# Waits between groups of four row scatters and gathers on GpSimd, in a kernel of two transformer layers with routed experts

## The chip, the cores and the metric

The kernel runs on one core of a Trainium2 chip. The metric is the device time of one execution in microseconds. A core has TensorE (PE in the profile), VectorE (DVE), ScalarE (ACT), GpSimd (POOL) and SyncE (SP), which run their own instruction queues in order and wait for each other on semaphores, and 16 DMA engines that all queues share.

## The reference

Input is x, 8 sequences of 512 tokens of 128 values. Two layers follow, each `x = x + ga * attention(h)` and then `x = x + gb * ffn(h)`, with `h = layernorm(x) * (1 + c) + s`, where shifts, scales and gains come from a small matrix product of a condition vector for each sequence.

- Layer 0: linear attention (16 heads of 8), then a mixture of 8 experts. For each token a softmax over 8 logits gives the two largest; each chosen expert computes `gelu(xn @ W1 + b1) @ W2 + b2` with 512 hidden values, and the two results are summed with normalised weights.
- Layer 1: softmax attention (8 heads of 16, each with values of 128 columns, the heads summed), then 8 experts of one 128x128 matrix, of which each token takes one.

The reference computes all experts for all tokens and masks. The kernel sorts the tokens by expert instead.

## The kernel before, in words

All work is in pairs: four pairs of two sequences, 1024 tokens, held as 8 row tiles of 128 tokens (NT = 8). Stages have names of kind.pair.part, and the order of the stages on every engine is written out by hand in the table ORDERS, one list for each engine (PE, ACT, DVE, POOL, and SP for the DMAs that SyncE issues). An engine takes its list in order; a stage that waits holds up all that stand behind it on this engine.

For the two-expert layer of pair i:

- VectorE computes, from TensorE's ranks (brk), the slot of each token and choice in a sorted buffer (posi, L1144). 23 tiles of 128 slots, each of one expert, hold the 2048 rows.
- bsc.i.0 to bsc.i.3 on GpSimd (L690): 16 indirect DMAs, four in each part, write the rows of z2 into xs (slots_in) in HBM, 128 rows of 512 bytes each. Each adds 16 to sc_out as it lands.
- bxl.i.j on SyncE (L530): waits until all 16 have landed (`sc_out >= 256 * (i + 1)`) and loads four tiles back. bw (L521) loads one expert's weights for each tile from the same in-order queue.
- bxt (transpose, L1496), bh (first product, L1503; gelu on ScalarE, L846), by (second product, L1511; copy on ScalarE, L854) on TensorE.
- byo (L540) stores the results to yd (slots_out) in HBM; bga.i.0 to bga.i.3 on GpSimd (L701): 16 indirect DMAs, four in each part, gather the rows back into yt, and count in ga_in[j], one semaphore for each part.
- bcm.i.j on VectorE (L1150, L1155) waits for ga_in[j] and combines; bcb (L1163, L1164) adds to x. Then come cn1 to cn4 (norms, partly on GpSimd: L658 to L665, L707, L708), and attention of layer 1: cpq (L1526), cpt on GpSimd (L736, L737), cto and cst (store and load of the split terms), s1 (L1538), mx on VectorE (L1198), s2 (L1554), exp on ScalarE (L887), pv (L1564).

For the one-expert layer, pairs 0 and 1 together go the same way: rsc.0.0 to rsc.0.3 (L722) scatter 16 blocks, rxl (L577) loads, rxt and rdx compute, rga.0.0 to rga.0.3 (L730) gather. Pairs 2 and 3 compute all experts (dx, L1607) and mask.

GpSimd's list has, around the parts: bsc.0.0 bn1.1.0 bsc.0.1 bsc.0.2 bsc.0.3; bsc.1.0 to bsc.1.3, then bga.0.0 to bga.0.3; bsc.2.0 bsc.2.1 bsc.2.2 bn1.3.0 bsc.2.3 cn1.0.0; bga.1.0 to bga.1.3, cpt.0.0; bsc.3.0 bsc.3.1 bsc.3.2 cpt.2.0 bsc.3.3, then bga.2.0 to bga.2.3, cpt.3.0; bga.3.0 to bga.3.3; rsc.0.0 to rsc.0.3, cpt.7.0; rga.0.0 rga.0.1 dx.2.0 rga.0.2 dx.2.2 rga.0.3. In the kernel before, only part 0 of a stream waits for anything; within a part and between the parts the DMAs are issued one behind the other.

Of the kernel before, what the change touches and what calls it, by code (L numbers as in the profile page):

```python
# [259 lines left out]
def build(nc, io, out):  # L260
    ctx = ExitStack()
    with ctx:
# [5 lines left out]
        def sem(name):  # L268
            return ctx.enter_context(nc.semaphore(name))
# [148 lines left out]
        def slot_rows(buf, g, n):  # L418
# [20 lines left out]
        ga_in = [sem(f"b_gathered{k}") for k in range(4)]  # L439
# [12 lines left out]
        r_row, r_mod, r_oh, r_rank, r_et, r_pos, r_sc, r_xt, r_mm, r_sum, r_wd = (  # L452
            sem("r_" + n) for n in ("rows_in_psum", "modulated", "one_hot", "ranks", "tile_experts", "slots", "scattered", "slots_turned",
                                    "expert", "x", "weights_stored"))
# [149 lines left out]
        def _(p):  # L604
# [41 lines left out]
            for kind, i, j in ORDER["POOL"]:  # L646
# [33 lines left out]
                if kind == "bsc":  # L680
                    if j == 0:
                        p.wait_ge(b_pos, i + 1)
                        p.wait_ge(b_z, i + 1)
                        if i == 0:
                            p.wait_ge(zx, 32)
                        if i >= 2:
                            p.wait_ge(b_xt, TG * (i - 1))
                    for x in range(4 * j, 4 * j + 4):
                        k, t = divmod(x, NT)
                        nc.gpsimd.indirect_dma_start(  # L690
                            xs[i % 2], bass.IndirectOffsetOnAxis(ap=posi[i][:, k, t:t + 1], axis=0),
                            z2[:, t, :], None).then_inc(sc_out, 16)
                if kind == "bga":
                    if j == 0:
                        for k in range(2):
                            p.wait_ge(ys_out[k], 16 * 3 * (i + 1))
                        if i:
                            p.wait_ge(b_cb, i)
                    for x in range(4 * j, 4 * j + 4):
                        t, k = divmod(x, 2)  # L700
                        nc.gpsimd.indirect_dma_start(  # L701
                            yt[:, k, t, :], None, yd[i % 2],
                            bass.IndirectOffsetOnAxis(ap=posi[i][:, k, t:t + 1], axis=0)).then_inc(ga_in[j], 16)
# [12 lines left out]
                if kind == "rsc":  # L716
                    if j == 0:
                        p.wait_ge(r_pos, 1)
                        p.wait_ge(r_mod, 2)
                    for x in range(4 * j, 4 * j + 4):  # L720
                        k, t = divmod(x, NT)
                        nc.gpsimd.indirect_dma_start(  # L722
                            xs[0], bass.IndirectOffsetOnAxis(ap=posi[0][:, k, t:t + 1], axis=0), zr[:, k, t, :], None).then_inc(r_sc, 16)
# [618 lines left out]
        def _(pe):  # L1342
# [10 lines left out]
            def keep_busy_aside(us, it):  # L1353

                _, gr, c = next((k for k in ORDER["PE"][ORDER["PE"].index(it):] if k[0] == "pv"), ("pv", len(values) // NC, 0))
                if c:
                    for _ in range(int(us / .23)):
                        nc.tensor.matmul(bank(7), nothing, rows, start=False, stop=False)
                else:
                    if gr:  # L1360
                        pe.wait_ge(c_ot, gr)
                    keep_busy(us, bank(7))
# [289 lines left out]
```

## Time and profile before

| | us |
|---|---|
| median of 3 runs | 782.74 |
| the runs | 777.67, 782.74, 787.64 |
| the profiled execution | 778.94 |
| its span, first to last instruction | 777.2 |
| busy: TensorE, VectorE, ScalarE, GpSimd | 632.0, 471.4, 392.1, 328.8 |
| mean granted TensorE clock | 0.905 |

The profiled execution is one of the program; what lies around its span is 1.7 us. Busy times are of instructions; waits, branches and DMA issues of SyncE do not count. "Releaser" is what ended a wait by the profile's semaphore events; "remote", and in the chain "another core or an unknown queue", stand where no instruction that fits was found. "Issue" is idle time for which no releaser is seen. Indirect DMAs stand as instructions of GpSimd, with the time in which it makes the descriptors, not that of the transfer. The matmuls of f32 operands stand as two instructions each. PEclk, the granted clock, is a share of 2.4 GHz; the other level, 1.2 GHz, is 0.50.

### The profile page before, as it was taken

To read this page: it belongs to the slowest core of one execution; us is meant where nothing else is said; L and a number is where in the kernel's file an instruction comes from. 1 tells how busy PE (TensorE), PEld (TensorE's weight loads), DVE (VectorE), ACT (ScalarE), POOL (GpSimd) and SP (SyncE) were. 2 spreads that over 40 slices of the span, in tenths; PEclk is the share of its full clock that TensorE was granted. 3 is DMA by queue.
4 is the path that set the end of the run, shared out by engine and by line. 5 is a ranking of instruction groups with operands and counts; after the bars stand their busy time and mean duration, and the time that the engine had idled before them with its cause. 6 is when DMAs were issued, how large, how long until landed. Compare 5 with 4: busy or idle time off the path is not lost.

```text
span 777.2 us, 12004 instructions
## 1 busy us (share of the span) xinstructions
PE 632.0 (81%) x3825; PEld 395.8 (51%) x3825; DVE 471.4 (61%) x1275; ACT 392.1 (50%) x866; POOL 328.8 (42%) x363
## 2 busy tenths in 40 slices
PE   8979889759496984988573999967899939988974
PEld 5646479658486984766120668812233312442332
DVE  3498847503365412778361685466899727588897
ACT  3451338637253653557342876644775417655430
POOL 5112880540608734351474131361646461406523
PEclk9999989959788895999795999986999679999998
DMA  8100337636457793596344358610420422532021
GB/s 342 50 1 29 125 93 241 213 121 199 136 170 243 243 322 94 198 297 184 129 143 114 90 189 269 224 41 14 150 82 2 132 87 78 171 99 65 14 54 27
DMA packets 47806, 106.41 MB, mean 137 GB/s; under 512 B 7825, under 2 KB 22993, under 8 KB 46209
## 3 DMA queue, kind: packets, MB, share of 16 engines
q1 hardware_dynamic: 42192, 94.82, 38.2%
q0 software_dynamic: 5120, 10.50, 4.3%
q8 instruction: 31, 0.51, 0.3%
q10 hardware_dynamic: 432, 0.34, 0.2%
q14 instruction: 31, 0.25, 0.1%
HBM read 80.26 MB, written 25.17 MB: 136 GB/s over the span
## 4 chain that ended last, share of the span: by engine, by line
PE 45%; DVE 18%; another core or an unknown queue 13%; ACT 9%; issue 7%; DMA 3%; POOL 2%; SPq 2%; DVEq 0%; ACTq 0%; POOLq 0%
PE PS L1503 8%; PE PS L1511 7%; DVE mxs L1198 6%; PE PS L1564 5%; PE PS L1554 4%; PE PS L1538 4%; ACT bufa L887 3%; ACT bufb L846 3%; DMA bufb<-in_experts_dram 3%; PE PS L1351 2%; PE PS L1607 2%; PE PS L1526 2%; PE PS L1427 1%; PE PS L1496 1%
## 5 line engine op out<-in xcount | busy, mean ns | idle before, releaser
L1198 DVE TENSOR_REDUCE mxs<-PS 128x2 f32<-128x1024 f32 x128 | 151.7, 1219 | 81.4 <-PE PS L1538 43.5
L887 ACT ACTIVATE bufa<-PS 128x512 f32<-128x512 f32 x256 | 140.8, 601 | 111.0 <-remote 49.5
L846 ACT ACTIVATE bufb<-PS,bufb 128x128 f32<-128x128 f32 x368 | 102.7, 378 | 99.5 <-PE PS L1503 50.2
L1503 PE MATMUL PS<-bufb 128*128 128x128 f32 x736 | 104.2, 292 | 22.8 <-issue 11.7
L1511 PE MATMUL PS<-bufb 128*128 128x128 f32 x736 | 102.5, 289 | 19.2 <-ACT bufb L846 10.1
L1554 PE MATMUL PS<-stk 108*128 108x512 bf16 x256 | 88.5, 404 | 35.1 <-ACT bufa L887 30.3
L1503 PEld LDWEIGHTS PS<-bufb 128*128 128x128 f32 x736 | 95.9, 204 | 33.6 <-issue 18.4
L1511 PEld LDWEIGHTS PS<-bufb 128*128 128x128 f32 x736 | 95.3, 203 | 24.0 <-ACT bufb L846 12.7
L1538 PE MATMUL PS<-stk 96*128 96x512 bf16 x256 | 81.2, 404 | 28.8 <-issue 10.2
L690 POOL DMA_INDIRECT slots_in<-bufb x64 | 66.3, 1037 | 70.6 <-DVE bufb L1144 52.7
L701 POOL DMA_INDIRECT bufb<-slots_out,bufb x64 | 61.0, 954 | 59.4 <-issue 33.8
L1554 PEld LDWEIGHTS PS<-stk 108*128 108x128 bf16 x256 | 23.3, 99 | 106.8 <-ACT bufa L887 63.4
L1564 PE MATMUL PS<-bufa,vv 128*32 128x512 f32 x512 | 74.2, 654 | 0.3 <-ACT bufa L894 0.2
L1538 PEld LDWEIGHTS PS<-stk 96*128 96x128 bf16 x256 | 20.6, 100 | 72.8 <-DVE mxs L1198 27.8
L1351 PE MATMUL PS<-identb 128*128 128x512 bf16 x187 | 46.2, 393 | 2.2 <-POOL dm L614 2.2
L656 POOL TENSOR_TENSOR rstd<-rstd,mhalf 128x8 f32<-128x8 f32 x12 | 20.7, 1725 | 62.4 <-DVE rstd L972 62.3
L736 POOL CAST terms<-rest 128x1024 bf16<-128x1024 f32 x8 | 8.3, 1043 | 72.7 <-DVE rest L1184 72.7
L1607 PE MATMUL PS<-bufb 128*128 128x512 f32 x64 | 30.6, 605 | 2.9 <-DVE bufb L1310 2.5
L838 ACT ACTIVATE bufb<-PS,cols 128x512 f32<-128x512 f32 (+1 forms) x24 | 18.5, 770 | 25.7 <-PE PS L1496 19.6
L1351 PEld LDWEIGHTS PS<-identb 128*128 128x128 bf16 x187 | 18.9, 102 | 22.0 <-issue 3.5
L658 POOL TENSOR_TENSOR mom<-st 128x16 f32<-128x16 f32 x11 | 2.4, 216 | 60.9 <-DVE st L956 60.9
L1035 DVE SCALAR_TENSOR_TENSOR bufa<-bufa 128x512 f32<-128x512 f32 x8 | 5.2, 686 | 35.4 <-ACT bufa L808 35.4
(292 smaller groups left out, 983.1 us busy)
## 6 DMA issues: line engine op xcount, KB each, us to landing
bufb<-in_experts_dram SPq DMA_DIRECT2D x92, 514.0 KB
stk<-split SPq DMA_DIRECT2D x96, 128.0 KB
slots_out<-bufb SPq DMA_DIRECT2D x30, 256.0 KB, 2.4
bufb<-slots_in SPq DMA_DIRECT2D x25, 256.0 KB, 4.1
split<-terms SPq DMA_DIRECT2D x8, 768.0 KB
slots_in<-hb SPq DMA_DIRECT2D x2, 1536.0 KB, 9.8
X<-in_x_dram SPq DMA_DIRECT2D x4, 512.0 KB, 6.5
out_dram<-X SPq DMA_DIRECT2D x6, 256.0 KB, 3.5
```

The costliest lines, as they stand in the source:

```text
L690: nc.gpsimd.indirect_dma_start(xs[i % 2], bass.IndirectOffsetOnAxis(ap=posi[i][:, k, t:t + 1], axis=0), z2[:, t, :], None).then_inc(sc_out ...
L701: nc.gpsimd.indirect_dma_start(yt[:, k, t, :], None, yd[i % 2], bass.IndirectOffsetOnAxis(ap=posi[i][:, k, t:t + 1], axis=0)).then_inc(ga_ ...
L846: last = nc.scalar.activation(hs[:, n % HR, fc, :], ps[:, P * fc:P * fc + P], ACT.Gelu_apprx_tanh, bias=ws[:, n % WR, F + fc:F + fc + 1])
L887: nc.scalar.activation(probs[:, i % PR, j, :], psum("s2", i, j), ACT.Exp, scale=DH1 ** -0.5)\
L1198: nc.vector.tensor_reduce(mxs[:, gr % 2, 2 * j:2 * j + 2, h], psum("s1", i, j).rearrange("p (c n) -> p c n", c=2), axis=AX.X, op=ALU.max)\
L1351: nc.tensor.matmul(place, identb[:, :], rows, start=True, stop=True)
L1503: last = nc.tensor.matmul(ps[:, P * fc:P * fc + P], ws[:, n % WR, P * fc:P * fc + P], xq[:, q % 2, P * x:P * x + P], start=True, stop=True)
L1511: last = nc.tensor.matmul(y, hs[:, n % HR, fc, :], ws[:, n % WR, W2AT + D * fc:W2AT + D * fc + D], start=(fc == 0), stop=(fc == FC - 1))
L1538: last = nc.tensor.matmul(ps[:, S * (c % 2):S * (c % 2) + S], qst[b % 2][0:KS, h, P * c:P * c + P], kst[b % 2][0:KS, h, :], start=True, st ...
L1554: nc.tensor.matmul(ps, kst[b % 2][0:KM, h, P * c:P * c + P], qst[b % 2][0:KM, h, :], start=True, stop=True).then_inc(c_s2x, 1)
L1564: last = nc.tensor.matmul(bank(7)[32 * hh:32 * hh + 32, :], vv[:, b % 3, j, 4 * k + hh, :], probs[:, n % PR, hh, :], start=(j == 0), stop= ...
L1607: last = nc.tensor.matmul(ps[:, 512 * e2:512 * e2 + 512], xTd[i % 2][:, P * j:P * j + P], expT[:, 4 * e2:4 * e2 + 4, :].rearrange("p e d - ...
```

## The change

Three waits are added on GpSimd. The second, third and fourth part of a scatter of pairs 1 to 3 (bsc) wait until all DMAs of the stream so far have landed; the second to fourth part of each gather (bga) until the part before has; the second to fourth part of the last scatter (rsc) likewise. The first pair's scatter and the last gather (rga) are as before. Nothing else is changed.

```diff
--- before.py
+++ after.py
@@ -685,6 +685,8 @@
                             p.wait_ge(zx, 32)
                         if i >= 2:
                             p.wait_ge(b_xt, TG * (i - 1))
+                    elif i:
+                        p.wait_ge(sc_out, 256 * i + 64 * j)
                     for x in range(4 * j, 4 * j + 4):
                         k, t = divmod(x, NT)
                         nc.gpsimd.indirect_dma_start(
@@ -696,6 +698,8 @@
                             p.wait_ge(ys_out[k], 16 * 3 * (i + 1))
                         if i:
                             p.wait_ge(b_cb, i)
+                    else:
+                        p.wait_ge(ga_in[j - 1], 64 * (i + 1))
                     for x in range(4 * j, 4 * j + 4):
                         t, k = divmod(x, 2)
                         nc.gpsimd.indirect_dma_start(
@@ -717,6 +721,8 @@
                     if j == 0:
                         p.wait_ge(r_pos, 1)
                         p.wait_ge(r_mod, 2)
+                    else:
+                        p.wait_ge(r_sc, 64 * j)
                     for x in range(4 * j, 4 * j + 4):
                         k, t = divmod(x, NT)
                         nc.gpsimd.indirect_dma_start(
```

## Rows read from the trace of the kernel before

**Rows 1.** The page: TensorE's busy time; the chain that ended last, by engine.
```profile
...
PE 632.0 (81%) x3825; PEld 395.8 (51%) x3825; DVE 471.4 (61%) x1275; ACT 392.1 (50%) x866; POOL 328.8 (42%) x363
...
PE 45%; DVE 18%; another core or an unknown queue 13%; ACT 9%; issue 7%; DMA 3%; POOL 2%; SPq 2%; DVEq 0%; ACTq 0%; POOLq 0%
...
```

**Rows 2.** View of waits: engine and line, releaser, us in total, times, longest.
```profile
...
ACT bufa L887 <- remote: 49.5, 10, 13.5
ACT bufb L846 <- remote: 45.7, 7, 11.9
...
```

**Rows 3.** Timeline, ScalarE and VectorE: start, us, what [idle before, releaser].
```profile
...
155.71 0.67 ACT L838 ACTIVATE bufb<-PS,cols 128x384 f32<-128x384 f32 x1 [5.36 <-remote]
...
169.29 1.14 ACT L846 ACTIVATE bufb<-PS,bufb 128x128 f32<-128x128 f32 x4 [11.88 <-remote]
...
215.03 1.23 DVE L1063 TENSOR_TENSOR bufa<-PS,modb 128x1024 f32<-128x1024 f32 x1 [11.42 <-remote]
...
707.45 1.23 DVE L1198 TENSOR_REDUCE mxs<-PS 128x2 f32<-128x1024 f32 x1 [2.22 <-remote]
...
```

**Rows 4.** Timeline of TensorE: what those at 169.29 and 215.03 need.
```profile
...
156.44 2.08 PE L1503 MATMUL PS<-bufb 128*128 128x128 f32 x8 [4.59 <-ACT bufb L838]
...
201.74 3.75 PE L1454 MATMUL PS<-wa,xTa 128*128 128x128 f32 x16 [4.20 <-issue]
...
```

**Rows 5.** Timeline of GpSimd: single indirect DMAs.
```profile
...
99.31 0.96 POOL L690 DMA_INDIRECT slots_in<-bufb  x1 [0.30 <-issue]
...
147.70 0.96 POOL L690 DMA_INDIRECT slots_in<-bufb  x1 [0.30 <-issue]
...
165.37 0.95 POOL L690 DMA_INDIRECT slots_in<-bufb  x1 [0.30 <-issue]
...
235.09 2.06 POOL L690 DMA_INDIRECT slots_in<-bufb  x1 [0.30 <-issue]
...
286.87 0.94 POOL L701 DMA_INDIRECT bufb<-slots_out,bufb  x1 [0.30 <-issue]
...
710.08 0.96 POOL L730 DMA_INDIRECT bufb<-slots_out,bufb  x1
...
```

**Rows 6.** Timeline of SyncE's DMA queue and of VectorE: who waits for rows.
```profile
...
101.54 7.43 SPq L530 DMA_DIRECT2D bufb<-slots_in  x4
...
182.47 0.85 SPq L530 DMA_DIRECT2D bufb<-slots_in  x2
...
292.76 0.67 DVE L1150 SCALAR_TENSOR_TENSOR bufb<-bufb,hb 128x128 f32<-128x128 f32 x2 [17.80 <-DMA bufb<-slots_out,bufb]
...
318.00 2.02 DVE L1150 SCALAR_TENSOR_TENSOR bufb<-bufb,hb 128x128 f32<-128x128 f32 x2
...
```

**Rows 7.** Stretches: length, busy PE, PEld, DVE, ACT, POOL, granted clock, DMA share, GB/s.
```profile
...
422.00:506.00 84.00, 81.33 (x579) 58.02 (x579) 50.41 (x102) 62.84 (x154) 20.24 (x24) 0.96 0.57 179
...
146.00:171.00 25.00, 12.90 (x79) 11.80 (x78) 2.42 (x4) 5.92 (x20) 15.41 (x16) 0.75 0.48 163
192.00:215.00 23.00, 11.87 (x75) 11.01 (x74) 7.67 (x34) 6.67 (x12) 15.09 (x16) 0.74 0.43 140
231.00:256.00 25.00, 18.34 (x123) 17.28 (x123) 14.28 (x34) 10.33 (x32) 20.14 (x22) 0.83 0.76 242
283.00:307.00 24.00, 11.91 (x81) 11.35 (x79) 2.04 (x8) 6.89 (x19) 15.21 (x16) 0.76 0.45 154
365.00:383.00 18.00, 9.68 (x55) 2.89 (x53) 6.97 (x10) 7.15 (x13) 11.53 (x12) 0.84 0.57 190
394.00:422.00 28.00, 12.01 (x54) 3.15 (x53) 7.81 (x13) 6.12 (x11) 19.47 (x21) 0.69 0.60 178
506.00:532.00 26.00, 15.82 (x66) 3.53 (x67) 14.67 (x20) 9.34 (x18) 15.31 (x16) 0.78 0.15 41
618.00:641.00 23.00, 10.74 (x46) 3.12 (x50) 5.27 (x5) 4.50 (x9) 15.50 (x16) 0.72 0.35 108
697.00:717.00 20.00, 17.28 (x86) 5.01 (x86) 16.70 (x25) 11.02 (x21) 14.99 (x15) 1.00 0.17 44
...
```

## The prediction

> **What bounds the kernel now.** I read the page first: its busy shares, then its chain. TensorE is busy for 632.0 of 777.2 us, and no other engine is near that; the chain goes through TensorE for 45%, and for 13% through "another core or an unknown queue", though there is one core [rows 1]. 13.2% of 777.2 us is about 102 us, so that name has to be found. The view of waits gives it as "remote": ScalarE alone waited 49.5 us in 10 waits before its exp (L887) and 45.7 us in 7 waits before its gelu (L846) [rows 2]. The timeline tells when. I filtered it for "remote": 30-odd waits, and every one of them lies inside, or within 5 us behind, a run of indirect DMAs on GpSimd (the row scatters and gathers); none lies between 424 and 506, where GpSimd issues none. The reader is to see four of them [rows 3]: ScalarE's L838 at 155.71 after 5.36 us, a gelu at 169.29 after 11.88 us, VectorE's L1063 at 215.03 after 11.42 us, and a short one at 707.45.
>
> What they waited for had been computed. The gelu of 169.29 waits for eight matmuls of L1503 that began at 156.44 and took 2.08 us; L1063 of 215.03 waits for the projection of L1454, which began at 201.74 and took 3.75 us [rows 4]. So the matmuls were over at 158.5 and 205.5, and the news of it took 10.8 and 9.5 us. GpSimd's runs lie exactly there: 16 scatters from 146.34 (the second is at 147.70) to 165.37, which is one every 17.67 / 14 = 1.26 us [rows 5], and 16 gathers that end at 211.7. The waits end 1 to 4 us behind the last issue. My reading: while row moves follow each other without a pause, what TensorE signals to other engines comes late; I can't say through what.
>
> Two things show that a pause lets the signals through. The scatter of the first pair and that of the third are broken up: single issues last 1.8 to 2.06 us there (as at 235.09 [rows 5]) and GpSimd has other work in between; from 76 to 101 ScalarE has no remote wait, from 231 to 256 two short ones, 4.64 and 1.87 us. And the last gathers (L730) come as eight, then 2.8 us of sums, then four from 710.08 [rows 5]: during the eight there is a wait of 2.22 us [rows 3], during the four none. The lateness begins some 4 us into a run, at its fourth DMA: in the run of 146.34 the first remote wait is that which ends at 155.71, so it began at 150.35.
>
> The Trainium skill (SBUF — State Buffer, "SBUF: two separate sides") says that a DMA cannot be slowed by a compute op, and vice versa. By that rule the 102 us would have another cause and the change would give nothing: it is the second rival below. The trace does not follow it in this case, since the waits come and go with the runs.
>
> **What the change removes.** The windows price it [rows 7]. Eight runs, each with its tail (146:171, 192:215, 231:256, 283:307, 365:383, 394:422, 506:532, 618:641), last 192 us together, and TensorE is busy in them for 12.90 + 11.87 + 18.34 + 11.91 + 9.68 + 12.01 + 15.82 + 10.74 = 103.3 us: 88.7 us idle. Two rows say what would be left without the lateness. In the stretch 422:506 without row moves, TensorE is idle for 2.7 of 84 us, 3%: of 192 us that is 6 us, an upper end of 83 us gained. In 697:717, with the gathers in a group of eight and one of four, it is idle for 2.7 of 20 us, 13.6%: of 192 us 26 us, so 63 us gained. I take the second, since it is the row nearest to groups of four.
>
> The clock comes on top. The granted clock is 0.69 to 0.84 in the eight windows and 0.96 and 1.00 in the two others [rows 7]: TensorE falls from 2.4 to 1.2 GHz after it stood idle, and goes on at the lower level for some us. 103.3 us of busy time at a mean of 0.76 would be some 103.3 x (1 - 0.76 / 0.96) = 21 us shorter at most; half of it, 10 us, is my estimate, because part of the low clock falls on idle time and the exps and VectorE's maxima don't get faster. Bounds 0 and 21 us.
>
> **What it adds.** Waits in front of the second, third and fourth group: 3 for each scatter of pairs 1 to 3, 3 for each of the four gathers, 3 for the last scatter (L722): 24, of which the one before bsc.3.3 costs nothing, since 12 us of other work lie in front of it. Each puts a landing in the place of a pitch of 1.26 us. The lower end of a landing: the last scatter of the first pair starts at 99.31, and SyncE, which waits for all 256, issues its load at 101.54 [rows 5, 6]: 2.2 us, so 1.0 us more for each wait, 3 us for a run. The upper end: the fourth gather of pair 1 starts at 286.87 and VectorE, which waits for those four, starts at 292.76 [rows 5, 6]: 5.9 us, 4.6 us more a wait, 14 us a run. That one lies amid weight loads and amid the lateness itself, so I take 1.3 us: 23 x 1.3 = 30 us of waiting on GpSimd, 4 us a run. Those 30 us are not on the path by themselves. Behind a waiting bsc or bga on GpSimd's queue stand: the rest of that stream, bn1.3 and cn1.0 behind the third scatter (VectorE waits for their pow), cpt.0 behind the second gather, cpt.7 behind the last scatter. Who waits for the rows: SyncE's bxl, VectorE's bcm.
>
> Their slack: bxl.1.0 is issued at 182.47 [rows 6], 15 us after its last scatter landed (165.37 + 2.2); VectorE's bcm.1.1 begins at 318.00 [rows 6], 14 us after the last of its gathers landed (286.87 + 12 x 1.25 + 2.2 = 304). But this slack is in large part the stall: with TensorE 9 to 12 us further on, 2 to 5 us are left, and the run ends 4 us later, in bad cases 14. So I charge 0 to 2 us in each of the eight places and 15 us in all; bounds 0 and 40 us (five places at 8 us). The first pair's scatter is not touched, nor the last gathers. The gather of pair 2 (bga.2.0) still starts without a wait right behind bsc.3.3, a run of eight: about 4 us of lateness stays there, and is inside the 26 us.
>
> **The sum.** 63 + 10 - 15 = 58 us less. The profiled execution took 778.94 us with a span of 777.2, and would take 721; it lies 3.8 us under the median of the three runs shown, 782.74. On the median's level: 725 us. Its own range, from the bounds that go together: gain 83 + 21 - 5, 99 us, gives 684; gain 63 + 0 - 35 gives 755.
>
> **Rivals.** First: the pause is too short. What GpSimd pauses is one landing, about 1 us in which nothing is issued, where the gap before 710.08 was 2.8 us and the work between the parts of the scatter of 76 to 101 lasted 2 us. Then the groups run together for the signals, and only a third of the 63 us comes: 21 - 15, about 6 us, with the longer runs sharing the lateness: 777. For it: full recovery behind the long runs took up to 1.8 us after the landing. Against it: the single issue of 2.06 us at 235.09, only 1.1 us longer than usual, is enough for the gelus behind it. In between lies a half effect, 745 to 765.
>
> Second: the runs aren't the cause, the same minutes of the kernel would be slow for another reason (weights landing late), and the change does not do what it says. Then only the charge of the waits is left, 0 to 15 us: 790, no change within 2%. Against it: in 506:532 the DMA share is 0.15 and TensorE is idle for 10 us all the same [rows 7].
>
> Third, on the other side: the landings take the place of the stall. A landing under load is 5.9 us [rows 6], not 2.2; each run of 16 then lasts 20 + 3 x 4.6, 34 us, and SyncE's in-order queue, where all weight loads stand behind a bxl, waits for the scatters. It decides from the point where a run grows by more than its slack of some 15 us of now, or sooner if the lateness goes on beside the waits. Five of eight runs at 8 us and a fifth of the gain (14 us): 782.7 + 40 - 14, about 809.
>
> The Trainium skill (DMA: Bandwidth & Descriptors, "Rules for kernel authors") speaks against the change: issue the DMA early, wait on its semaphore late, the fixed cost overlaps; and it gives some 2.0 us of fixed cost for a DMA from GpSimd (section "Anatomy of one DMA"). The fixed cost agrees with the 2.2 us of [rows 5, 6]. By the rule alone the change would only add 23 waits, which is the third rival at its lower prices.
>
> **Chances.** My forecast 0.74 (684 to 755); half effect or too short a pause 0.14 (745 to 777); not the cause 0.06; landings instead of the stall 0.06. The range that should hold it 8 times in 10 reaches from 692 to 765. 2% of 782.74 is 15.7 us, about what a measurement of this kernel can tell from no change: faster below 767. Faster 0.86 (the forecast, and most of the half effect), same 0.08, slower 0.06.
>
> **What the profile after would show.** Remote waits in the view of waits fall from over 100 us to under 30, and "another core" in the chain from 13% to under 4%. GpSimd's timeline shows groups of four 1.26 us apart and a gap of 1.1 to 2 us (plus the 0.3) before the fifth, ninth and thirteenth. The PEclk line has no falls to 7 in those slices, and mean clock rises from 0.905 to about 0.95. TensorE's idle time in each former window is 2 to 4 us. I am wrong if these waits stay while the gaps are there (first rival), if they stay elsewhere (second), or if VectorE's L1150 and SyncE's L530 now wait for landings by 5 us or more each (third).

## The result and the profile after

The kernel with the waits takes 723.65 us (median of 4 runs, 718.42 to 729.92), that without them 782.62 us (4 runs, 777.67 to 787.64) on the same chip. The ratio is 0.9212 with a 95% interval of 0.9148 to 0.9275: faster by 8%. The profiled execution of after is the longest of its four, 729.92 us with a span of 728.2 us; that of before was 3.7 us under its median. So the two profiles stand 49.0 us apart in span and the medians 59.0 us, and everything read below accounts for the 49.

I read the page first: the span, TensorE's busy time, the granted clock in 40 slices and the chain.

```profile
span 728.2 us, 12004 instructions
...
PE 621.5 (85%) x3825; PEld 390.0 (54%) x3825; DVE 483.3 (66%) x1275; ACT 391.9 (54%) x866; POOL 328.6 (45%) x363
...
PEclk9999999999998899889998999999999699999998
...
PE 19%; DVE 11%; issue 5%; POOL 5%; DMA 4%; SPq 4%; ACT 1%; ACTq 0%; DVEq 0%; POOLq 0%
```

TensorE is busy for 10.5 us less than in [rows 1] (632.0) with the same 3825 matmuls, which I put down to the clock. It is idle for 106.7 us where it was 145.2: 38.5 us less. The two make the 49.0. "Another core or an unknown queue" is gone from the chain; but this chain reaches back only to 368.4 us, so it shows one half of the kernel, and the view of waits is the safer place. There the change shows from both sides (engine, line, tile, what it waited for: us in total, times, longest):

```profile
POOL bufb L705 <- DMA bufb<-slots_out,bufb: 36.5, 12, 4.5
...
POOL slots_in L692 <- DMA slots_in<-bufb: 28.0, 8, 5.3
...
DVE bufb L1156 <- DMA bufb<-slots_out,bufb: 25.5, 5, 9.5
...
PE PS L1509 <- DMA bufb<-in_experts_dram: 13.9, 6, 6.0
...
DVE mxs L1204 <- remote: 7.9, 4, 4.2
ACT bufb L844 <- remote: 7.8, 3, 2.8
...
ACT bufb L852 <- remote: 6.4, 4, 3.5
...
POOL slots_in L728 <- DMA slots_in<-bufb: 4.6, 3, 1.5
...
ACT bufb L860 <- remote: 3.8, 1, 3.8
...
ACT stk L886 <- remote: 3.2, 1, 3.2
...
ACT bufa L900 <- remote: 2.1, 1, 2.1
```

The lines marked "remote" sum to 31.2 us. In before the same lines sum to 165.9 us, 95.2 of them in the two of [rows 2] (the gelu is L852 now, the exp L893, which has none left). In exchange GpSimd stands at 23 of the 24 added waits for 36.5 + 28.0 + 4.6 = 69.1 us, 3.0 us each. Other landings are waited for longer. VectorE's first combine (now L1156) waited 17.8 us in one piece before [rows 6], and TensorE waited for expert weights 3.0 us, which are 13.9 now:

```profile
PE PS L1503 <- DMA bufb<-in_experts_dram: 3.0, 3, 1.7
```

(that is the same view of before; the matmul is L1509 after). One wait for a landing is new. VectorE's second norm (L986, called at L1091) writes the rows z2 of pair 2 over those that the scatters of pair 1 still read, so it waits until they have landed, and TensorE waits for it in turn:

```profile
177.72 2.14 DVE L986 TENSOR_SCALAR bufb<-hb,mom,rstd 128x128 f32<-128x128 f32 x8 [6.08 <-DMA slots_in<-bufb]
...
180.00 1.94 PE L1466 MATMUL PS<-identf,bufb 128*128 128x128 f32 x8 [5.82 <-DVE bufb L986]
```

The timeline shows the new rhythm of GpSimd, and where the last "remote" waits lie (start, duration, engine, line; in brackets the idle time before and its releaser):

```profile
150.42 0.96 POOL L692 DMA_INDIRECT slots_in<-bufb  x1 [0.30 <-issue]
...
155.09 0.96 POOL L692 DMA_INDIRECT slots_in<-bufb  x1 [3.71 <-DMA slots_in<-bufb]
...
163.72 0.96 POOL L692 DMA_INDIRECT slots_in<-bufb  x1 [3.89 <-DMA slots_in<-bufb]
...
212.26 0.94 POOL L705 DMA_INDIRECT bufb<-slots_out,bufb  x1 [0.30 <-issue]
213.51 1.31 POOL L692 DMA_INDIRECT slots_in<-bufb  x1 [0.30 <-issue]
...
215.68 0.58 ACT L860 COPY bufb<-PS 128x512 f32<-128x512 f32 x1 [3.85 <-remote]
```

ScalarE's operations of 155.71 (L838) and 169.29 (a gelu), which had waited 5 and 12 us [rows 3], have no such wait near them; the one "remote" wait of that stream is of 0.72 us, at 160.85. The one of 215.68 lies where the last four gathers of pair 0 (208.52 to 212.26) and the first four scatters of pair 2 (213.51 on) meet without a wait: a run of eight is left there. The windows follow, one for each of the eight streams with its tail and a quiet one (length, busy PE, PEld, DVE, ACT, POOL, granted clock, DMA share, GB/s), to be laid beside [rows 7]:

```profile
146.00:179.00 33.00, 25.12 (x198) 23.60 (x197) 6.17 (x16) 20.86 (x52) 15.41 (x16) 0.99 0.66 207
183.00:215.00 32.00, 27.60 (x218) 25.16 (x216) 21.59 (x80) 17.18 (x47) 17.32 (x17) 0.96 0.70 227
215.00:247.00 32.00, 25.55 (x183) 23.56 (x183) 9.82 (x24) 16.04 (x51) 17.83 (x24) 0.89 0.64 204
265.00:299.00 34.00, 31.51 (x230) 27.70 (x228) 11.51 (x42) 21.46 (x55) 17.70 (x18) 0.95 0.55 189
356.00:383.00 27.00, 21.71 (x104) 6.69 (x98) 18.96 (x23) 15.20 (x29) 18.66 (x18) 0.94 0.34 114
383.00:406.00 23.00, 18.46 (x111) 12.15 (x112) 13.41 (x24) 15.47 (x34) 13.10 (x14) 0.85 0.58 160
472.00:497.00 25.00, 21.05 (x114) 6.63 (x114) 22.06 (x40) 14.07 (x26) 14.09 (x15) 1.00 0.14 36
576.00:599.00 23.00, 19.52 (x93) 5.65 (x92) 13.85 (x20) 12.51 (x23) 14.36 (x15) 0.89 0.38 115
...
407.00:470.00 63.00, 61.17 (x455) 45.73 (x454) 38.03 (x75) 43.93 (x116) 17.61 (x23) 1.00 0.68 221
```

In the eight, TensorE is busy for 190.5 of 229 us, so idle for 38.5; before it was idle for 88.7 of 192. The windows are longer because the streams are. They gave 50.2 us; outside them idle time grew from 56.5 to 68.2 us, which is 11.7 us given back.

Late signals are not all that goes with the runs. TensorE itself is held up in them. Behind the projection of L1454 [rows 4] its next matmuls of before come singly, with idle time for which no releaser is seen, while the gathers are issued:

```profile
210.47 0.37 PE L1503 MATMUL PS<-bufb 128*128 128x128 f32 x1 [1.83 <-issue]
...
212.61 0.37 PE L1503 MATMUL PS<-bufb 128*128 128x128 f32 x1 [1.76 <-issue]
...
214.00 0.37 PE L1503 MATMUL PS<-bufb 128*128 128x128 f32 x1 [1.03 <-issue]
```

All lines of the view of waits that give TensorE's matmuls the releaser "issue" sum to 43.2 us in before and to 15.1 us in after.

### The profile page after: what moved, and what is told of

Its sections match the earlier page's. It is cut to its first block and busy times, and to the rows that moved or that the text cites. A ratio compares the mean times of both kernels' runs of the same rounds, so it can differ in the third digit from the quotient of the medians.

```text
span 728.2 us, 12004 instructions
## 1 busy us (share of the span) xinstructions
PE 621.5 (85%) x3825; PEld 390.0 (54%) x3825; DVE 483.3 (66%) x1275; ACT 391.9 (54%) x866; POOL 328.6 (45%) x363
## 5 line engine op out<-in xcount | busy, mean ns | idle before, releaser
L893 ACT ACTIVATE bufa<-PS 128x512 f32<-128x512 f32 x256 | 140.5, 601 | 70.5 <-PE PS L1560 46.0
L852 ACT ACTIVATE bufb<-PS,bufb 128x128 f32<-128x128 f32 x368 | 102.9, 379 | 74.7 <-PE PS L1509 62.0
L1509 PE MATMUL PS<-bufb 128*128 128x128 f32 x736 | 105.4, 295 | 26.3 <-DMA bufb<-in_experts_dram 13.9
L1509 PEld LDWEIGHTS PS<-bufb 128*128 128x128 f32 x736 | 96.6, 206 | 38.0 <-issue 24.4
L692 POOL DMA_INDIRECT slots_in<-bufb x64 | 64.7, 1011 | 81.3 <-DVE bufb L1150 37.3
L1560 PE MATMUL PS<-stk 108*128 108x512 bf16 x256 | 86.5, 396 | 17.3 <-ACT bufa L893 9.0
L1517 PE MATMUL PS<-bufb 128*128 128x128 f32 x736 | 98.1, 282 | 3.3 <-ACT bufb L852 2.5
L1517 PEld LDWEIGHTS PS<-bufb 128*128 128x128 f32 x736 | 91.5, 197 | 6.7 <-ACT bufb L852 4.3
L705 POOL DMA_INDIRECT bufb<-slots_out,bufb x64 | 62.1, 971 | 66.4 <-DMA bufb<-slots_out,bufb 36.5
L1570 PE MATMUL PS<-bufa,vv 128*32 128x512 f32 x512 | 71.8, 635 | 0.2 <-ACT bufa L900 0.2
L1357 PE MATMUL PS<-identb 128*128 128x512 bf16 x187 | 48.4, 408 | 2.2 <-POOL dm L614 2.2
L736 POOL DMA_INDIRECT bufb<-slots_out,bufb x16 | 15.4, 962 | 23.8 <-DMA slots_out<-bufb 19.5
L728 POOL DMA_INDIRECT slots_in<-bufb x16 | 15.5, 967 | 18.1 <-DVE bufb L1305 9.8
L1570 PEld LDWEIGHTS PS<-bufa,vv 128*32 128x32 f32 x512 | 10.5, 110 | 24.4 <-issue 21.8
```

The source lines that it names most:

```text
L692: nc.gpsimd.indirect_dma_start(xs[i % 2], bass.IndirectOffsetOnAxis(ap=posi[i][:, k, t:t + 1], axis=0), z2[:, t, :], None).then_inc(sc_out ...
L705: nc.gpsimd.indirect_dma_start(yt[:, k, t, :], None, yd[i % 2], bass.IndirectOffsetOnAxis(ap=posi[i][:, k, t:t + 1], axis=0)).then_inc(ga_ ...
L852: last = nc.scalar.activation(hs[:, n % HR, fc, :], ps[:, P * fc:P * fc + P], ACT.Gelu_apprx_tanh, bias=ws[:, n % WR, F + fc:F + fc + 1])
L893: nc.scalar.activation(probs[:, i % PR, j, :], psum("s2", i, j), ACT.Exp, scale=DH1 ** -0.5)\
L1357: nc.tensor.matmul(place, identb[:, :], rows, start=True, stop=True)
L1509: last = nc.tensor.matmul(ps[:, P * fc:P * fc + P], ws[:, n % WR, P * fc:P * fc + P], xq[:, q % 2, P * x:P * x + P], start=True, stop=True)
```

## Experiments

Each kernel is compared with the kernel before on the same chip. "Remote" is the sum of the lines with that name in the view of waits of its profiled execution; "landing waits" are GpSimd's own for its row moves. Times are medians, with the lowest and highest run in brackets. Unless a diff says otherwise, the edit is against the kernel after the change.

**Which streams carry the gain.** First the waits in the scatters of pairs 1 to 3 alone, the other two additions taken out.

```diff
                     elif i:
                         p.wait_ge(sc_out, 256 * i + 64 * j)     (kept)
-                    else:
-                        p.wait_ge(ga_in[j - 1], 64 * (i + 1))
-                    else:
-                        p.wait_ge(r_sc, 64 * j)
```

> Only the scatters of pairs 1 to 3 keep the waits; gathers and the last scatter run without. Lateness theory (an unbroken run of row moves on GpSimd holds up what TensorE signals): the stalls go in the three scatters alone, worth 12.1 + 6.7 + 8.3 of the 88.7 us of idle before, less what their waits cost: 760 to 770 us. If the gain came from one stream only (a rival), this one gives all of it (724) or nothing (783). Remote waits should be gone in the scatters and stand as before in the gathers.

764.13 us (762.65 to 768.3) against 776.28; ratio 0.9841 (0.9779 to 0.9903): 12 us. Remote 135.2 us, all of it but 0.15 us outside the three scatters. As expected.

Then the waits in the four gathers alone.

```diff
-                    elif i:
-                        p.wait_ge(sc_out, 256 * i + 64 * j)
                     else:
                         p.wait_ge(ga_in[j - 1], 64 * (i + 1))   (kept)
-                    else:
-                        p.wait_ge(r_sc, 64 * j)
```

> Only the four gathers keep the waits. Lateness theory: 11.1 + 12.1 + 16.0 + 10.2 us of idle time were theirs, 35 to 40 us come back: 743 to 750 us. Rival (the writes of the scatters into HBM are what holds up the signals): no gain, 780 us.

760.48 us (758.42 to 765.45), ratio 0.9807 (0.973 to 0.9885): 16 us, less than half of the 35 to 40 that I expected. Both ratios lie clear of 1, but neither interval lies wholly beyond 2%. Remote is down to 90.4 us, so the signals of the gathers come as foreseen; but VectorE's combine now waits for its rows:

```profile
DVE bufb L1152 <- DMA bufb<-slots_out,bufb: 45.2, 6, 28.6
```

17.8 us before [rows 6], 45.2 here. The lateness also moved on: the scatter of pair 2 follows the gather at once, still unbroken, and ScalarE's gelu at 240.25 waits 11.9 us there, where the longest such wait of this scatter was 4.6 us in before. Which of the two costs the gain was not run. The two parts give 28 us, the whole 59. The last scatter's waits alone were not run, so how much of the other 31 us is theirs and how much only comes when no stream is left unbroken stays open.

**Is it the number of row moves under way?** With groups of four that each wait for the last one, at most four are in flight. A gather may instead wait for the group before the last: up to eight in flight, and hardly a pause. Only the gathers have waits here.

```diff
-                    else:
-                        p.wait_ge(ga_in[j - 1], 64 * (i + 1))
+                    elif j > 1:
+                        p.wait_ge(ga_in[j - 2], 64 * (i + 1))
```

> Only the four gathers have waits, and each for the group before the last one (the third group waits for the first, the fourth for the second): no more than eight DMAs in flight, but hardly a pause. Compared with waits for the last group in the gathers alone (760, ratio 0.981). Pause theory: the first group has landed long before the third begins, GpSimd issues without a break, nothing is gained: 770 to 785 us. Rival (too many row moves in flight at once): as good as the waits in the gathers, 755 to 765 us.

778.21 us (771.67 to 784.03), ratio 0.9998 (0.9961 to 1.0035), remote 135.8 us. No landing wait of the gathers shows on GpSimd at all, the groups run together, and nothing is gained: where the waits hold nothing up, they are worth nothing. This remote sum is 30 us under that of before with the same span of 777.2 us, so differences of that size between two such sums mean little by themselves.

**How long may a group be?** A wait before every second row move, and one wait in the middle of the sixteen.

```diff
 groups of two (the same in the gather and in the last scatter)
                     for x in range(4 * j, 4 * j + 4):
+                        if i and x % 4 == 2:
+                            p.wait_ge(sc_out, 256 * i + 16 * x)
 groups of eight (the same in the gather and in the last scatter)
-                    elif i:
+                    elif i and j == 2:
                         p.wait_ge(sc_out, 256 * i + 64 * j)
```

> As the changed kernel, but a wait in front of every second DMA instead of every fourth. Lateness theory, with the lateness beginning some 4 us into a run: a run of 2 never gets there, so remote waits vanish, but GpSimd waits for 7 landings a stream instead of 3, some 2.7 us each, 11 us more a stream; I expect 720 to 735 us. If the lateness begins at once, groups of 2 gain further: under 715 us. If the longer streams are what ends last, over 740 us.

> As the changed kernel, but one wait only, in the middle of each stream. Lateness theory: each half of 10 us is stalled from its fourth us on, so about a third to a half of the gain stays: 745 to 760 us. If only the first pause mattered, or the number of landings per stream, it is 724 us; if a run of eight is as bad as one of sixteen, 775 us.

Groups of two: 777.13 us (773.85 to 781.11), ratio 1.0017 (0.9981 to 1.0052), no gain at all, where I had expected 720 to 735. Groups of eight: 739.82 us (737.13 to 741.03), ratio 0.9539 (0.9482 to 0.9597), a little better than expected. The first is the more telling. Its view of waits has not one "remote" line; what it has instead:

```profile
DVE bufb L1162 <- DMA bufb<-slots_out,bufb: 79.1, 13, 12.6
POOL bufb L709 <- DMA bufb<-slots_out,bufb: 74.5, 28, 6.5
...
POOL slots_in L694 <- DMA slots_in<-bufb: 49.4, 19, 5.1
...
PE PS L1515 <- DMA bufb<-in_experts_dram: 32.1, 7, 12.5
...
PE PS L1508 <- DMA bufb<-slots_in: 18.0, 3, 14.2
```

With another 11.9 us in the last scatter GpSimd is held up for 135.8 us in 54 waits. All 166 us of late signals are gone, and what the third rival foresaw stands in their place: rows land late for VectorE, and the queue behind SyncE's row loads lands late for TensorE. VectorE's second norm waits 16.4 us for the scatters, and the lines of TensorE with the releaser "issue" are down to 3.3 us. In groups of eight remote is 81.2 us and the landing waits are 20.6 us (7).

**Landing or pause?** In the next two nothing waits for a landing. GpSimd does one pow of 128x8 elements between the groups, into a tile that nobody reads, or two in a row.

```diff
+        idle = sb("idle", [P, NT])
...
                     elif i:
-                        p.wait_ge(sc_out, 256 * i + 64 * j)
+                        own.link(tt(idle[:, :], epst[:, :], mhalf[:, :], ALU.pow))
                     else:
-                        p.wait_ge(ga_in[j - 1], 64 * (i + 1))
+                        own.link(tt(idle[:, :], epst[:, :], mhalf[:, :], ALU.pow))
                     else:
-                        p.wait_ge(r_sc, 64 * j)
+                        own.link(tt(idle[:, :], epst[:, :], mhalf[:, :], ALU.pow))
```

> In the places of the added waits GpSimd does one power of a 128x8 tile, 1.65 us, and waits for its end; it waits for no landing. If a pause in the issuing is what lets TensorE's signals through, the remote waits fall nearly as far as in the changed kernel (31 us) and GpSimd is held up for 23 x 1.9 us instead of 69 us: 700 to 720 us. If it takes the landing (no row move in flight at some moment), which under load comes 3 to 5 us after the fourth, most of the gain in the weight-loading part is lost and the rest stays: 735 to 755 us.

> The same with two powers, 3.5 us. Pause theory: remote waits no higher than with one power, 23 x 1.8 us more on GpSimd, so equal to the changed kernel or slower: 710 to 725 us. Landing theory: now most landings fit into the pause and the time comes near to the changed kernel, 715 to 730 us, faster than with one power.

One pow: 701.91 us (698.56 to 704.12), ratio 0.9017 (0.8967 to 0.9068), below the interval of the change itself. Its page and GpSimd's timeline:

```profile
PE 613.3 (87%) x3825; PEld 384.4 (55%) x3825; DVE 476.7 (68%) x1275; ACT 391.8 (56%) x866; POOL 372.2 (53%) x387
...
PE 32%; POOL 19%; DVE 18%; issue 9%; DMA 7%; SPq 7%; ACT 6%; another core or an unknown queue 1%; DVEq 0%; POOLq 0%; ACTq 0%
```

```profile
148.14 0.96 POOL L694 DMA_INDIRECT slots_in<-bufb  x1 [0.30 <-issue]
149.13 1.68 POOL L691 TENSOR_TENSOR idle<-epst,mhalf 128x8 f32<-128x8 f32 x1
151.10 1.04 POOL L694 DMA_INDIRECT slots_in<-bufb  x1 [0.29 <-POOL idle L691]
```

From the end of the fourth issue to the start of the fifth it is 2.0 us (149.10 to 151.10) where the wait for the landing took 3.7 (151.38 to 155.09 in after). Remote is 17.1 us, not more than the 31.2 with the longer stop. So it is not the landing that helps; the landing is only a pause, and a dearer one than needed. The granted clock rises to 0.961.

Two pows: 742.69 us (741.8 to 743.68), ratio 0.9559 (0.9509 to 0.9608), where I had expected at most 730. Remote is 22.8 us, no better than with one. 24 pauses x 1.7 us are 41 us more on GpSimd, and the kernel is 40.8 us slower (TensorE is busy for 7 us of these, at a granted clock of 0.938): in this step a microsecond of stream cost about a microsecond. POOL is the largest share of its chain, 33%, and VectorE waits again:

```profile
DVE bufb L1160 <- DMA bufb<-slots_out,bufb: 38.8, 9, 9.7
```

**How short may the pause be, and how is it to be spread?** Three linked multiplications (0.78 us) in the place of the pow; the pow once in the middle of sixteen; and the short pause after every second row move, so that a stream has about as much pause as with the pow, in smaller pieces. The diffs are against the kernel with one pow.

```diff
 short pause
-                        own.link(tt(idle[:, :], epst[:, :], mhalf[:, :], ALU.pow))
+                        for _ in range(3):
+                            own.link(tt(idle[:, :], epst[:, :], mhalf[:, :], ALU.mult))
 pow in the middle alone
-                    elif i:
+                    elif i and j == 2:
 short pause every two: as the first, and
                     for x in range(4 * j, 4 * j + 4):
+                        if i and x % 4 == 2:
+                            for _ in range(3):
+                                own.link(tt(idle[:, :], epst[:, :], mhalf[:, :], ALU.mult))
```

> The pause of the kernel with one pow (1.68 us of work, 1.96 us from the end of the fourth issue to the start of the fifth, instead of 0.30) is cut to about half: three multiplications of 128x8 elements, 0.20 us each and linked, some 0.85 us, so 1.1 to 1.2 us between the groups. If any pause of about 1 us is enough for TensorE's signals, remote waits stay under 30 us and the shorter streams give another 0 to 10 us: 692 to 704. If the pause has to be near 2 us, remote waits come back to 50 to 120 us and the time is 715 to 750.

> One pow after the eighth row move of each stream instead of one after every fourth: the pause is the same, the runs between are 8 long. If lateness builds up from about the fourth DMA of a run, remote waits are near the 81 us of the kernel with one landing wait in the middle, GpSimd is held up for 10 us less than there, and the time is 725 to 740. If a pause as such is what counts, wherever it lies, remote waits are under 40 us and the time is 695 to 710.

> The short pause (three multiplications, 0.78 us of work) after every second row move instead of after every fourth. For 16 row moves this is 7 pauses of 0.78 us beside work, 0.76 us of extra gap each, 5.3 us, against 3 x 1.67 = 5.0 us in the kernel with one pow every four (701.9 us) and 2.3 us in that with the short pause every four (743.3 us, 92 us of remote waits). If lateness builds up with each row move and is paid back with the idle time of GpSimd's issue, whatever its form, remote waits are under 35 us and the time is 698 to 715. If a pause under 1 us gives nothing back and only long ones do, remote waits stay at 60 to 100 us and, with streams as long as with the pow, the time is 735 to 755.

Short pause every four: 743.34 us (740.42 to 747.02), ratio 0.9482 (0.9404 to 0.9559), remote 92.1 us; a gap of 1.08 us in place of 0.30 is too short for four row moves. Pow in the middle alone: 750.52 us (738.85 to 756.06), ratio 0.9605 (0.9524 to 0.9686), remote 81.7 us, as expected, but slower than my 725 to 740. One of its waits lies in the first eight gathers of pair 0 (182.02 to 191.8) and the pause behind them:

```profile
193.50 1.07 ACT L822 COPY xTa<-PS 128x512 f32<-128x512 f32 x2 [6.36 <-remote]
```

Short pause every two: 709.08 us (705.9 to 712.35), ratio 0.9094 (0.9019 to 0.9168). Its rhythm, and both of its "remote" lines:

```profile
147.76 0.96 POOL L697 DMA_INDIRECT slots_in<-bufb  x1 [0.30 <-issue]
148.73 0.79 POOL L695 TENSOR_TENSOR idle<-epst,mhalf 128x8 f32<-128x8 f32 x3
149.80 1.00 POOL L697 DMA_INDIRECT slots_in<-bufb  x1 [0.28 <-POOL idle L695]
```

```profile
ACT stk L899 <- remote: 3.1, 1, 3.1
...
DVE bufb L1329 <- remote: 0.7, 1, 0.7
```

The same short pause that left 92.1 us of late signals after every four leaves 3.8 us after every two. So it is not the length of the single pause that counts, but how much pause there is for how many row moves.

**The places that the change left out.** First the landing waits also in the scatter of pair 0, before the gather of pair 2, and in the last gather; then, against the kernel with one pow, a pow before the scatter and the gather of pair 2 and in the last gather.

```diff
 landing waits everywhere
-                    elif i:
+                    else:
                         p.wait_ge(sc_out, 256 * i + 64 * j)
 bga, j == 0
+                        if i == 2:
+                            p.wait_ge(sc_out, 1024)
 rga
+                    else:
+                        p.wait_ge(r_ga[(j - 1) // 2], 64 * ((j - 1) % 2 + 1))
 pow at the joins: in bsc and bga, j == 0
+                        if i == 2:
+                            own.link(tt(idle[:, :], epst[:, :], mhalf[:, :], ALU.pow))
 rga
+                    else:
+                        own.link(tt(idle[:, :], epst[:, :], mhalf[:, :], ALU.pow))
```

> The changed kernel with waits in the three places that it leaves out: the first pair's scatter, between the last part of the fourth scatter and the gather behind it, and the last gather. Theory: 4 to 8 of the 31 us of remote waits left lie behind the fourth scatter and go; the first pair's scatter has none to lose and starts everything behind it 6 to 9 us later, as no other expert work is there to hide it: 722 to 732 us against 717 to 724, slightly slower.

> Beside the pauses of the kernel with one pow every four, one at each place where two runs meet without one: before the scatter of pair 2 (behind the gather of pair 0), before the gather of pair 2 (behind the scatter of pair 3), and three in the last gather. If the remaining 17 us of remote waits come from those runs of eight, they fall under 10 us, and the time is 694 to 702; the last gather lies on the path, and its pauses (2 x 1.7 us) may take 3 us of it back: not over 706.

Landing waits everywhere: 724.43 us (723.52 to 725.25), ratio 0.9322 (0.9274 to 0.937); remote 10.8 us, landing waits 78.3 us (28). Pow at the joins: 705.73 us (700.62 to 708.28), ratio 0.902 (0.8956 to 0.9085); remote 10.7 us against 17.1. In both the late signals fall to some 11 us, and in neither does the time follow: the ratio of the second is that of one pow every four (0.9017), and its 706 us lie at my limit and not in the 694 to 702 that I had expected. The last places cost about what they give.

**The kernels that treat the eight streams alike, in one table.** "Added" is the time that a stream of sixteen grows by its pauses, each less the plain 0.30 us: for landing waits (69.1 - 23 x 0.30) / 23 = 2.7 us a wait in after, 2.6 in groups of eight, 2.2 in groups of two (135.8 us in 54 waits); for the others the gap in the timeline, 2.00 us with a pow, 1.08 with the short pause, 3.71 with two pows.

| kernel | added per stream, us | remote, us | ratio to before |
|---|---|---|---|
| before | 0 | 165.9 | 1 |
| pow in the middle | 1 x 1.7 = 1.7 | 81.7 | 0.9605 |
| short pause every 4 | 3 x 0.78 = 2.3 | 92.1 | 0.9482 |
| landing in the middle | 1 x 2.6 = 2.6 | 81.2 | 0.9539 |
| pow every 4 | 3 x 1.7 = 5.1 | 17.1 | 0.9017 |
| short pause every 2 | 7 x 0.78 = 5.5 | 3.8 | 0.9094 |
| landing every 4 (after) | 3 x 2.7 = 8.1 | 31.2 | 0.9212 |
| two pows every 4 | 3 x 3.4 = 10.2 | 22.8 | 0.9559 |
| landing every 2 | 7 x 2.2 = 15.5 | 0 | 1.0017 |

About 2 us added takes off half of the lateness, 5 us nearly all of it and a tenth of the time; within these two groups the ratios' intervals overlap, so no difference between the forms of the pause is shown. Beyond 5 us the time comes back with the stream's length. The change lies at 8 us, on the far side of the best.

## Why the prediction came right

**What bounds the kernel.** The reading was right. The "remote" waits belong to the unbroken runs of row moves: they went from 165.9 to 31.2 us with the runs cut, to 0 with runs of two, and stayed (135.8) when waits were there that held nothing up. I had said from over 100 to under 30. But "what TensorE signals comes late" was only part of it: TensorE's own idle time without a releaser goes the same way, 43.2 us before, 15.1 after, 7.6 with one pow every four, 3.3 in groups of two. By what path the row moves do this is still not shown, nor whether it is their issue on GpSimd or the transfers behind it; the runs show only that the delay comes and goes with unbroken issue. The Trainium skill (SBUF — State Buffer, "SBUF: two separate sides") holds that a DMA and a compute op can't slow each other; the costliest operations of ScalarE and VectorE did not get longer here (the exp 601 ns in both kernels, VectorE's maximum 1.22 us), but the news of one did come up to 12 us late [rows 3], so the rule is no ground for looking elsewhere.

**The gain in the eight windows.** 63 us forecast from the window of eight and four gathers, 50.2 measured (88.7 to 38.5 us idle). The idle time is 2.5 to 7.9 us a window, against the 2 to 4 that I gave. The first window owes 5.8 of its 7.9 us to the longer stream: TensorE stands from 174.2 on and waits for VectorE's L986, which waits for the scatters to land. I had not listed this among those that wait for the rows. The next largest, 6.5 and 5.3 us, hold a run of eight at a join (208.52 to 218.6 with its tail, 372.01 to 381).

**The clock.** 10 us forecast, 10.5 measured as less busy time for the same matmuls. This is a weak confirmation: the 10 was simply half of my bound of 21, and groups of two have nearly the same busy time (621.2 us against 621.5) at a granted clock of 0.916, so the 10.5 need not all be clock. The granted clock is 0.85 to 1.00 in the eight windows, 0.69 to 0.84 before [rows 7], and 0.946 over the span where I gave 0.95.

**The landings: the term that was mis-sized.** I priced a wait at 1.3 us over the plain pitch and took 30 us for 23 of them. It was 2.7 us each and 62 us in all: single waits of 1.5 us in the quiet last scatter, up to 5.3 us beside the weight loads. The value that I took came from the quiet row, 2.2 us [rows 5, 6], and the other end, 5.9 us, was set aside as amid weight loads and the lateness itself. The mean came out half way between the two: 4.0 us from the start of a group's last issue to the start of the next group. The gaps on GpSimd's timeline are 1.5 to 5.3 us, where my 1.1 to 2 plus the 0.3 would be 1.4 to 2.3.

**What longer streams cost.** 15 us charged; in the profile 11.7 us of idle time more outside the windows, and in the waits 7.7 us more for rows at VectorE (25.5 against 17.8) and 10.9 more for weights at TensorE (13.9 against 3.0). With the 5.8 us behind L986, which lie inside a window, that is 17.5. The charge fitted although the waits were twice as long, and that is luck: it was a guess of up to 2 us a place. But I had written that pauses "are not on the path by themselves", and that holds at most for the first few microseconds of a stream: from one pow to two, 41 us of pause cost 40.8 us. In the change itself the landing's extra 3.0 us a stream over a pow, 24 us in eight streams, goes with a ratio higher by 0.0195, some 15 us. That is how the slack of 14 to 15 us in [rows 6] has to be read: most of it was the stall, as I wrote, and what is left seems to be used up at about 5 us; between there and 8 us the price was 15 us for 24, and between 5 and 10 us about one to one.

**The sum.** 63 + 10 - 15 = 58 was forecast, 49.0 in the two profiles is 50.2 + 10.5 - 11.7, and 59.0 in the medians. For the profiled execution I had forecast 721 us, and it took 729.92: the windows gave 13 us less than forecast, the rest of the sum 4 us more. That the median came within 1.4 us of 725 is luck.

**The rivals.** The first (pause too short) fell for this change but is real: it is what the short pause every four (743 us) shows, with a gap of 1.08 us, the "about 1 us in which nothing is issued" of its text. Landings were dearer than I thought, and that kept the change clear of it: at my price a gap would have been 1.6 us, between those of the short pause (1.08 us, 743 us) and the pow (2.0 us, 702 us), where nothing was run. The second (another cause) fell with the table. The third did not decide here, but its signs are there in part. VectorE's combines wait 5.1 us each in five waits, and SyncE, which waited for scatters once (22.8 us) in before, does so three times:

```profile
SPq L530 <- DMA slots_in<-bufb: 40.2, 3, 22.8
```

So two of its row loads, with the weight loads behind them, wait 17.4 us more; I had named 5 us or more each as the sign that I was wrong by this rival, and the gain was large enough to outweigh it. In groups of two it cancels the whole gain. The rule of the Trainium skill named with it (DMA: Bandwidth & Descriptors, "Rules for kernel authors": issue early, wait late) does not hold for these streams: every kernel whose waits or pauses held GpSimd up by 2 to 10 us a stream beat the one that issues as early as it can. The fixed cost of 2.0 us that goes with it is the low end here: from the start of a group's last issue to the start of the next group it was 0.96 + 1.54 = 2.5 us in the last scatter and 0.96 + 5.3 = 6.2 us at 231.57.

## What to carry to other kernels

Where a single-core trace shows engines released by "remote" or by "another core", and those waits lie in or just behind a run of indirect DMAs on GpSimd, look for TensorE's matmuls that ended long before: the signals are late, and breaking up the run is worth trying early. Break it with a pause of known, short length (here one 1.7 us operation after every four row moves, 2.0 us in all, or other work that GpSimd has to do anyway) rather than with a wait for landings, whose length the memory traffic sets. List first everything that waits for the rows, buffers that are written over included. Then sweep pause and group size and watch both sides, the "remote" sum and the waits for the rows, since the best lies where the two meet (702 us here, 724 with landing waits, 777 with waits twice as many).

## What the runs showed of the hardware

- While row moves are issued 1.26 us apart in runs of eight or more, ScalarE and VectorE stand for up to 13.5 us [rows 2] before operations whose matmuls the profile shows as done, and TensorE's own matmuls come singly, with up to 1.8 us of idle time and no releaser before one (210.47). Time in which GpSimd issues none takes this back: 5 us added to a stream of sixteen leaves 4 to 17 us of the 166, whether as three pauses or as seven; 2 us leaves 81 to 92.
- It doesn't matter that GpSimd is busy in the pause: a pow in the middle of sixteen leaves 81.7 us of late signals, standing still for the landing there 81.2.
- The wait for four row moves to land was 1.5 us in the stretch with a DMA share of 0.38 (576:599) and up to 5.3 us in one with 0.64 (215:247) of the same kernel.
